# A GRU recurrence inside a fused kernel: state as the stationary operand, W_hh streamed in four column tiles, tanh in place of sigmoid

## The reference, cut to what matters

```python
# layer 0, quantised on both sides
gate = mx_linear(x, w_gate); up = mx_linear(x, w_up)
x1 = x0 + mx_linear(silu(gate) * up, w_down)
# layer 1, the recurrence (B=16, T=256, D=512)
def cell(h, x):
    gi = x @ W_ih + b_ih
    gh = h @ W_hh + b_hh
    r = sigmoid(i_r + h_r); z = sigmoid(i_z + h_z)
    n = tanh(i_n + r * h_n)
    return (1.0 - z) * n + z * h
# layer 1, router: silu hidden layer, top 2 of 16 by softmax, then base + experts
```

## Time and profile before

| | |
|---|---|
| three timed runs | 1957.7, 1959.59, 1968.15 us; median 1959.59 |
| span of the profiled execution, first to last instruction | 1957.8 us (its own time is not listed apart; it is within 2 us of the median) |
| TensorE busy | 1641.2 us (84%) |
| VectorE busy | 1636.9 us (84%) |
| ScalarE, GpSimd busy | 635.5 and 643.7 us (32%, 33%) |
| the 256 steps | 238.4 to 1936.2 us |

### The profile page before, as it was taken

The page is one execution under the profiler, slowest core; times in us unless marked ns, Lnnn a source line. Parts: engine busy times, 40 slices in busy tenths (PEclk is TensorE's granted clock), DMA queues, the critical chain, the costliest instruction groups (busy, mean ns, idle before and its releaser), DMA issues. The chain is left out here.

```text
span 1957.8 us, 82261 instructions
## 1 busy us (share of the span) xinstructions
PE 1641.2 (84%) x32972; PEld 1251.9 (64%) x32972; DVE 1636.9 (84%) x5843; ACT 635.5 (32%) x1711; POOL 643.7 (33%) x795
## 2 busy tenths in 40 slices
PE   5422347999999999999999999999999999999976
PEld 2211115776777777777777777777777777777764
DVE  8999887888888888888888888888888888887653
ACT  1111223433333333333333333333333333333331
POOL 4545323333333333333333332333333333332111
PEclk8755568999999999999999999999999999999997
DMA  7313120000000000000000000000000000000100
GB/s 264 135 59 124 40 97 23 25 30 31 22 19 27 30 30 30 30 30 30 30 30 29 26 30 30 30 30 30 30 30 30 27 17 24 30 25 27 33 14 18
DMA packets 35405, 80.45 MB, mean 41 GB/s; under 512 B 4864, under 2 KB 5248, under 8 KB 34688
## 3 DMA queue, kind: packets, MB, share of 16 engines
q1 hardware_dynamic: 28080, 63.09, 9.6%
q10 hardware_dynamic: 6992, 12.13, 1.8%
HBM read 58.43 MB, written 16.78 MB: 38 GB/s over the span
## 5 line engine op out<-in xcount | busy, mean ns | idle before, releaser
L1294 PE MATMUL ps_rn<-hx,whh 128*128 128x32 f16 x16384 | 451.2, 176 | 85.0 <-DVE hx L715 47.4
L1294 PEld LDWEIGHTS ps_rn<-hx,whh 128*128 128x128 f16 x16384 | 430.9, 96 | 129.8 <-DVE hx L715 90.3
L1016 POOL COPY hT_steps<-hx 128x128 f16<-128x128 f16 x256 | 120.2, 469 | 992.3 <-DVE hx L715 992.3
L1187 PE MATMUL ps_gi<-x1T,wih 128*128 128x128 f16 x4608 | 289.6, 219 | 1.2 <-ACT gi L523 1.2
L1187 PEld LDWEIGHTS ps_gi<-x1T,wih 128*128 128x128 f16 x4608 | 271.3, 98 | 25.9 <-issue 1.7
L532 ACT ACTIVATE r<-r_pre,scale 128x64 f32<-128x64 f32 x256 | 89.0, 348 | 581.6 <-DVE r_pre L735 581.6
L1294 PE MATMUL ps_z<-hx,whh 128*128 128x32 f16 x8192 | 244.2, 176 | 0.0
L1294 PEld LDWEIGHTS ps_z<-hx,whh 128*128 128x128 f16 x8192 | 223.5, 96 | 0.1
L523 ACT ACTIVATE gi<-ps_gi,b_i,scale_x 128x128 f32 (+1 forms) x384 | 144.4, 456 | 159.1 <-PE ps_gi L1187 159.1
L1003 POOL TENSOR_TENSOR qf<-f8c,fe 128x512 bf16<-128x512 bf16 x128 | 135.8, 1061 | 148.4 <-DVE f8c L796 148.4
L1120 PE MATMUL ps_gate_up<-wq,qxT 128*128 128x512 bf16 x512 | 143.6, 397 | 19.5 <-issue 15.0
(11 more groups left out here) (198 smaller groups left out, 2885.2 us busy)
## 6 DMA issues: line engine op xcount, KB each, us to landing
wih<-in_x_steps ACTq DMA_DIRECT2D x32, 256.0 KB, 5.5
xin<-in_x_steps SPq DMA_DIRECT2D x32, 256.0 KB, 4.0
xres<-in_x_steps SPq DMA_DIRECT2D x32, 256.0 KB, 4.1
x_dram<-x SPq DMA_DIRECT2D x32, 256.0 KB, 2.9
x_in<-x_dram SPq DMA_DIRECT2D x32, 256.0 KB, 2.7
out_rows<-y SPq DMA_DIRECT2D x32, 256.0 KB, 2.0
wst<-in_ffn_w SPq DMA_DIRECT2D x12, 512.0 KB, 3.4
sg_gs<-in_ffn_w SPq DMA_DIRECT2D x12, 512.0 KB, 3.7
```

The lines of the kernel that those rows point to most:

```text
L1016: g.tensor_copy(hT_steps[:, :, s, :], hx[:, :, :, :].rearrange("p k u b -> p (k u) b"))\
L1187: last = mm(ps_gi[:, j * P:(j + 1) * P], wih_parts[:, k, at:at + P], x1T[:, x, k, :], start=k + w + x == 0, stop=k == KD - 1 and w == 1)
L1294: last = mm(ps[:, (at + j) * 2 * B:(at + j + 1) * 2 * B], whh[:, k, u, gate * D + j * P:gate * D + (j + 1) * P], hx[:, k, :, :].rearrange( ...
```

## The change

`state_products` swaps the operands. The 32 columns of `hx` for one chunk of depth are now stationary, in one of four groups of 32 columns of TensorE's array, and W_hh streams past: one product writes 32 partitions of the bank, 256 columns for r and n together and 128 for z. That is 32 products for r and n and 32 for z, 64 a step. The sums now lie sequence on partition, in blocks of 32x32, so VectorE turns them with a 32x32 block transpose from PSUM into `rn_turned` and `z_turned` before it adds. The bias of n's recurrent part is laid out beside r's share in `gi`, so that one pair of additions of 128 columns serves r and n.

`sigmoid(a)` becomes `(1 + tanh(a/2)) / 2`, with the halves folded into scales and into `scalar_tensor_tensor` operations. In the recurrence the z sums now stand ahead of `rn` on VectorE, and z's tanh ahead of n's on ScalarE. In the feed-forward net and the router one silu on ScalarE takes the place of a sigmoid on ScalarE and a product on VectorE. The router's softmax share becomes a tanh and two small GpSimd operations. Some buffers of the weight preparation share memory with later ones.

```diff
--- before.py
+++ after.py
+GI_PARTS = 4
+GI_AT = {GATE_N: 0, GATE_Z: 1, GATE_R: 2}
+GI_BIAS = 3
+GROUPS = P // 32
...
-        gi = sb("gi", [P, 2 * 3 * STEPS * HB])
+        gi = sb("gi", [P, 2 * GI_PARTS * D])
         h = sb("h", [P, HB])
         hx = sb("hx", [P, KD, 2, B], F16)
-        r_half, r_pre, z_half, z_pre = (sb(x, [P, HB]) for x in ("r_half", "r_pre", "z_half", "z_pre"))
-        hn_half, hn, r, z = (sb(x, [P, HB]) for x in ("hn_half", "hn", "r", "z"))
-        rn, n_pre, n, n_scaled, nmh, zd = (sb(x, [P, HB]) for x in ("rn", "n_pre", "n", "n_scaled", "nmh", "zd"))
+        rn_turned, z_turned = sb("rn_turned", [P, 2, KD, 2, B]), sb("z_turned", [P, KD, 2, B])
+        rn_half, rn_pre = sb("rn_half", [P, 2, KD, B]), sb("rn_pre", [P, 2, KD, B])
+        z_half, z_pre = sb("z_half", [P, HB]), sb("z_pre", [P, HB])
+        r_tanh, z_tanh, rn, n_pre, n = (sb(x, [P, HB]) for x in ("r_tanh", "z_tanh", "rn", "n_pre", "n"))
+        less_z, zh, zn = (sb(x, [P, HB]) for x in ("less_z", "zh", "zn"))
...
+        def gi_r_and_bias(c, s):
+
+            if isinstance(c, int):
+                at = (c % 2 * GI_PARTS + GI_AT[GATE_R]) * D
+                part = gi[:, at:at + 2 * D]
+            else:
+                part = gi[:, bass.ds((c & 1) * (GI_PARTS * D) + GI_AT[GATE_R] * D, 2 * D)]
+            return part.rearrange("p (q k n) -> p q k n", q=2, k=KD)[:, :, :, s * B:(s + 1) * B]
...
-                    nc.scalar.activation(hid_sg[:, :], hid_pre[:, :], ACT.Sigmoid).then_inc(hs_ok, 1)
+                    nc.scalar.activation(hid[:, :], hid_pre[:, :], ACT.Silu).then_inc(hid_ok, 1)
...
-                    wait(act, gs_done, count(f, NF, s // 2))
-                    nc.scalar.activation(sg[:, :], ps_gate[:, :], ACT.Sigmoid).then_inc(sg_done, 1)
+                    wait(act, inter_done, count(f, NF, s // 2))
+                    nc.scalar.activation(gs, ps_gate[:, :], ACT.Silu).then_inc(gs_done, 1)
...
-                    act.wait_ge(r_pre_ok, t1)
-                    nc.scalar.activation(r[:, :], r_pre[:, :], ACT.Sigmoid, scale=S_INV).then_inc(r_ok, 1)
+                    act.wait_ge(rn_pre_ok, t1)
+                    nc.scalar.activation(r_tanh[:, :], rn_pre[:, 0, :, :], ACT.Tanh, scale=HALF_S_INV).then_inc(r_ok, 1)
+                    act.wait_ge(z_pre_ok, t1)
+                    nc.scalar.activation(z_tanh[:, :], z_pre[:, :], ACT.Tanh, scale=HALF_S_INV).then_inc(z_ok, 1)
                     act.wait_ge(n_pre_ok, t1)
-                    nc.scalar.activation(n[:, :], n_pre[:, :], ACT.Tanh, scale=S_INV).then_inc(n_ok, 1)
-                    act.wait_ge(z_pre_ok, t1)
-                    nc.scalar.activation(z[:, :], z_pre[:, :], ACT.Sigmoid, scale=S_INV).then_inc(z_ok, 1)
+                    nc.scalar.activation(n[:, :], n_pre[:, :], ACT.Tanh, scale=HALF_S_INV).then_inc(n_ok, 1)
...
-                r_both, n_both, z_both = (ps.rearrange("p (k u b) -> p k u b", k=KD, u=2) for ps in
-                                          (ps_rn[:, 0:2 * HB], ps_rn[:, 2 * HB:4 * HB], ps_z[:, 0:2 * HB]))
                 if s == 0:
                     dve.wait_ge(gi_ev, count(c, 3, 3))
                 dve.wait_ge(rn_mm, t1)
-                v.tensor_tensor(by_chunk(r_half[:, :]), r_both[:, :, 0, :], gi_step(c, GATE_R, s),
-                                ALU.add).then_inc(r_half_ok, 1)
-                v.tensor_tensor(by_chunk(hn_half[:, :]), n_both[:, :, 0, :],
-                                b_h[:, 2 * KD:3 * KD].unsqueeze(2).broadcast_to([P, KD, B]),
-                                ALU.add).then_inc(hn_half_ok, 1)
-                dve.wait_ge(r_half_ok, t1)
-                v.tensor_tensor(by_chunk(r_pre[:, :]), r_both[:, :, 1, :], by_chunk(r_half[:, :]),
-                                ALU.add).then_inc(r_pre_ok, 1)
-                dve.wait_ge(hn_half_ok, t1)
-                v.tensor_tensor(by_chunk(hn[:, :]), n_both[:, :, 1, :], by_chunk(hn_half[:, :]),
-                                ALU.add).then_inc(hn_ok, 1)
+                v.transpose(rn_turned[:, :, :, :, :], ps_rn[:, 0:4 * HB]).then_inc(rn_turn_ok, 1)
+                dve.wait_ge(rn_turn_ok, t1)
+                v.tensor_tensor(rn_half[:, :, :, :], rn_turned[:, :, :, 0, :], gi_r_and_bias(c, s),
+                                ALU.add).then_inc(rn_half_ok, 1)
+                dve.wait_ge(rn_half_ok, t1)
+                v.tensor_tensor(rn_pre[:, :, :, :], rn_turned[:, :, :, 1, :], rn_half[:, :, :, :],
+                                ALU.add).then_inc(rn_pre_ok, 1)
                 beside(1)
-                dve.wait_ge(hn_ok, t1)
+                dve.wait_ge(z_mm, t1)
+                v.transpose(z_turned[:, :, :, :], ps_z[:, 0:2 * HB]).then_inc(z_turn_ok, 1)
+                dve.wait_ge(z_turn_ok, t1)
+                v.tensor_tensor(by_chunk(z_half[:, :]), z_turned[:, :, 0, :], gi_step(c, GATE_Z, s),
+                                ALU.add).then_inc(z_half_ok, 1)
+                dve.wait_ge(z_half_ok, t1)
+                v.tensor_tensor(by_chunk(z_pre[:, :]), z_turned[:, :, 1, :], by_chunk(z_half[:, :]),
+                                ALU.add).then_inc(z_pre_ok, 1)
+                dve.wait_ge(rn_pre_ok, t1)
                 dve.wait_ge(r_ok, t1)
-                v.tensor_tensor(rn[:, :], r[:, :], hn[:, :], ALU.mult).then_inc(rn_ok, 1)
-                dve.wait_ge(z_mm, t1)
-                v.tensor_tensor(by_chunk(z_half[:, :]), z_both[:, :, 0, :], gi_step(c, GATE_Z, s),
-                                ALU.add).then_inc(z_half_ok, 1)
+
+                v.scalar_tensor_tensor(by_chunk(rn[:, :]), by_chunk(r_tanh[:, :]), 1.0, rn_pre[:, 1, :, :], ALU.add,
+                                       ALU.mult).then_inc(rn_ok, 1)
                 dve.wait_ge(rn_ok, t1)
-                v.tensor_tensor(by_chunk(n_pre[:, :]), by_chunk(rn[:, :]), gi_step(c, GATE_N, s),
-                                ALU.add).then_inc(n_pre_ok, 1)
-                dve.wait_ge(z_half_ok, t1)
-                v.tensor_tensor(by_chunk(z_pre[:, :]), z_both[:, :, 1, :], by_chunk(z_half[:, :]),
-                                ALU.add).then_inc(z_pre_ok, 1)
+                v.scalar_tensor_tensor(by_chunk(n_pre[:, :]), gi_step(c, GATE_N, s), 2.0, by_chunk(rn[:, :]), ALU.mult,
+                                       ALU.add).then_inc(n_pre_ok, 1)
                 beside(2)
                 wait(dve, hcopy, c * STEPS + s)
 
+                dve.wait_ge(z_ok, t1)
+                v.tensor_scalar(less_z[:, :], z_tanh[:, :], 1.0, HALF_S_H, ALU.subtract, ALU.mult)
+                v.scalar_tensor_tensor(zh[:, :], z_tanh[:, :], 1.0, h[:, :], ALU.add, ALU.mult).then_inc(zh_ok, 1)
+                dve.wait_ge(zh_ok, t1)
                 dve.wait_ge(n_ok, t1)
-                v.scalar_tensor_tensor(nmh[:, :], n[:, :], S_H, h[:, :], ALU.mult, ALU.subtract).then_inc(nmh_ok, 1)
-                v.tensor_scalar(n_scaled[:, :], n[:, :], S_H, None, ALU.mult)
-                dve.wait_ge(nmh_ok, t1)
-                dve.wait_ge(z_ok, t1)
-                v.tensor_tensor(zd[:, :], z[:, :], nmh[:, :], ALU.mult).then_inc(zd_ok, 1)
-                dve.wait_ge(zd_ok, t1)
-                v.tensor_tensor(hx[:, :, 0, :], by_chunk(n_scaled[:, :]), by_chunk(zd[:, :]),
-                                ALU.subtract).then_inc(hx_hi, 1)
-                v.tensor_tensor(h[:, :], n_scaled[:, :], zd[:, :], ALU.subtract).then_inc(h_ok, 1)
+                v.tensor_tensor(zn[:, :], less_z[:, :], n[:, :], ALU.mult).then_inc(zn_ok, 1)
+                dve.wait_ge(zn_ok, t1)
+                v.scalar_tensor_tensor(hx[:, :, 0, :], by_chunk(zh[:, :]), 0.5, by_chunk(zn[:, :]), ALU.mult,
+                                       ALU.subtract).then_inc(hx_hi, 1)
+                v.scalar_tensor_tensor(h[:, :], zh[:, :], 0.5, zn[:, :], ALU.mult, ALU.subtract).then_inc(h_ok, 1)
                 low_part(t1 + 1)
...
-                        dve.wait_ge(sg_done, count(f, NF, s // 2 + 1))
-                        v.tensor_tensor(gs[:, :], ps_gate[:, :], sg[:, :], ALU.mult).then_inc(gs_done, 1)
...
+                    for place, sign in enumerate((0.5, -0.5)):
+                        g.tensor_scalar(share[:, place:place + 1], gap_tanh[:, :], sign, 0.5, ALU.mult,
+                                        ALU.add).then_inc(share_ok, 1)
...
-            def state_products(ps, at, gate):
-
-
-                for j in range(KD):
+            def state_products(ps, gates):
+
+                n = len(gates) * P
+                step = gates[-1] - gates[0] + 1
+                for w in range(2):
                     for k in range(KD):
-                        for u in range(2):
-                            last = mm(ps[:, (at + j) * 2 * B:(at + j + 1) * 2 * B],
-                                      whh[:, k, u, gate * D + j * P:gate * D + (j + 1) * P],
-                                      hx[:, k, :, :].rearrange("p u b -> p (u b)"), start=k + u == 0,
-                                      stop=k + u == KD)
```

(11 more changed lines are left out.)

83 lines of the change are left out of this document (48 added, 35 removed).

## The result

The changed kernel takes 2117.46 us (median of 4 runs, 2115.9 to 2119.9) against 1960.26 of the kernel before, run beside it: a ratio of 1.0799, 95% interval 1.0775 to 1.0824. It is 157 us slower. The forecast said slower, by 55, with a range of 1905 to 2095: the direction came true, the time lies outside the range. One execution among all that follow stands apart, 7475.56 us in run 12, where the nine others took 1949.0 to 1957.7; no cause of it is known, and the ratio given there leaves it out.

What follows compares the result with a forecast made beforehand. TensorE and VectorE were taken to be late in turns, VectorE in steps 3 to 7. Looped tiles +50, written-out tiles +12 and start-up -7 gave +55 on 1959.6, so 2015 us, range 1905 to 2095.

Steps and rivals of the forecast that it cites:

- the steps across the branch: Steps 7 and 0, going by TensorE through the loop's branch: 13.4 us together against 13.91 before.
- the gap between dependent operations: On VectorE, 0.04 us taken between an operation and the one that depends on it.
- What bounds it: TensorE and VectorE late in turns, VectorE in steps 3 to 7; TensorE's products to take 1.0 (r, n) and 0.8 (z).
- One of the signs: In the profile after, VectorE was to be busy above 90% of a looped tile.
- The transposes and the chain: VectorE's turns at 0.42 and 0.28 us, its chain 3.41 from rn_turned to line 715: +0.35 in every step.
- two passes: Rival: each transpose costs 0.26 and 0.14 more per step, 3.2 a tile, 2095 us in all; chance 0.12.
- the column groups did overlap: Rival, that they don't: TensorE's products take 5.1 to 6.1 a step instead of 2.4, 2600 us or more; chance 0.05.
- The waits for GpSimd: VectorE sums with two SBUF inputs held by GpSimd: step 3 7.6 against 6.45, step 7 6.0 against 5.6, step 5 +0.15.
- The rival in which the waits don't come: VectorE's sums are not held by GpSimd: step 3 5.45, a tile 50.9, 1935 us or 1900; chance 0.25.
- The small operations and the router: beside(1)'s operations uncovered, two more GpSimd operations for the share: step 4 6.55 against 5.54, step 6 7.9 against 6.54.
- The sum: A looped tile of 53.7 us against 51.7, +2.0 a tile, over 25 looped tiles +50.
- The start-up: Ahead of the tiles, gs leaves the chain: some 7 us less.

Runs made afterwards that it cites:

- run 12: The changed kernel with all tiles written out instead of looped and the transposes' results in PSUM: 1953.22 us, 0.997 of the kernel before.
- run 10: The changed kernel with its loop over 12 pairs of tiles, so that which half of gi is read is a constant: 2034.98 us, ratio 1.038.
- run 5: The changed kernel with 21 additional one-column memsets at VectorE's start, moving its loop body from 939 to 960 in the instruction stream: 2052.74 us, ratio 1.0479.
- run 1: The changed kernel with both transposes writing to unused columns of their PSUM banks instead of SBUF: 2092.31 us, ratio 1.0678 to the kernel before.
- run 9: The kernel before with 107 additional one-column memsets ahead of VectorE's program, so that its loop body begins at 1067 instead of 960: 1983.14 us, ratio 1.0132.
- run 11: The kernel before, written out, with one silu operation in place of the gate's sigmoid and product: 1856.1 us, 0.9476 of the kernel before.

## Why the prediction was wrong, and what held of it

The direction and most of the mechanism held, the size did not: +157 against +55. In the forecast's own terms, two of them were mis-sized, both by what a hardware loop costs: the steps across the branch, 13.4 forecast and 15.69 measured, which is the larger, and the gap between dependent operations, 0.04 forecast and 0.14 measured behind three operations a step.

**What bounds it.** Right: VectorE is late in nearly all steps, and TensorE's relief pays little. The wait for r and n fell from 106.8 to 22.3 us, and `ps_rn` starts z after 0.88 and ends after 1.06, near the forecast 1.0. z takes 0.5 to 0.6, below the 0.8 that I took and within its bounds. One of the signs failed: VectorE was to be busy above 90% of a looped tile and is busy 84% (919 of 1100 us), since the gaps behind dependent operations and the jump are idle time. Written out it is 92%.

**The transposes and the chain.** Right in length, 0.44 and 0.31 against 0.42 and 0.28, and 3.38 against 3.41 for the chain, but only in the kernel written out. The Trainium skill, "VectorE: DVE Perf Modes", section "The three transpose paths", has 311 ns for 128x128 in bf16; this trace has 306 for fp32, and the runs have nothing in bf16 beside it. There were no two passes, and the column groups did overlap: those rivals are out.

**The first step that failed: "between dependent ones I take 0.04".** That holds (0.034) only where the operation's address is a constant. Where an operation in the loop reads `gi`, 0.14 lie between it and its forerunner, and the change put three such operations one behind another (`rn_half`, `z_half`, `n_pre`). The term is 0.2 to 0.3 in most steps, 1.7 a tile, some 40 us over 25 tiles (run 10 against run 5). No row of the kernel before shows it, since no operation that reads `gi` follows there directly on the one it waits for: `z_half` stands between `rn` and `n_pre`.

**The second and larger one: the steps across the loop's branch, "13.91 - 0.6 - 0.6 + 0.67 = 13.4".** I took the branch as a fixed 1.41 on TensorE that VectorE does not have. In fact each engine has its own, and it is long when the engine fetches its loop anew. The change shortened TensorE's loop from 2080 instructions (130 KB) to 1568 (98 KB); it is no longer fetched anew, and the 1.41 of "issue" ahead of step 0's products is gone. VectorE's shrank too, from 302 to 295, but moved from 960 to 939 in the stream, and has been fetched anew since. Measured: 15.69 for steps 7 and 0, 2.3 above the forecast, and 0.35 more in step 4. With VectorE's loop moved back by 21 instructions they take 13.35, and the kernel 2052.74 (run 5). That 13.35 meets the forecast's 13.4 is in part luck: the forecast went by TensorE through a branch of 1.41, and what was measured is VectorE through a loop without one, with the address gaps in it.

**The waits for GpSimd.** Right in kind and place: 7.6 was forecast for step 3 and 7.83 measured, with three operations held. That the size fits so well is luck, as the three were not the ones I named. `f8c` did not get in ahead of `xg` but came 0.02 late, and so `rn_turned` started 2.5 after the step's beginning and not 1.6, and `z_half` passed free. The rival in which the waits don't come is out by run 1.

**The small operations and the router.** Step 4 was to be 6.55 and step 6 7.9; written out they are 6.31 and 7.79, and the loop adds 0.9 and 0.3; of the 0.9, 0.35 goes with the long jump (run 5). In step 6 two `share` operations of 0.33 on GpSimd stand ahead of `c`, and `wxa` waits 0.55 for `coeff`, which comes behind it.

**The sum.** With VectorE's loop in a short place a tile is 55.0 against the 53.7 forecast: the address term of 1.7 is missing, while the other terms of steps 3 to 6 had been taken 0.06 to 0.24 too long (written out 7.54, 6.31, 6.26 and 7.79 against 7.6, 6.55, 6.5 and 7.9). The sum's 11.75 for steps 1 and 2 was given without its working; it is 12.2 in the loop and 11.45 written out. The start-up, forecast 7 shorter, is 10 shorter at the end of tile 0's first step (330.1 against 339.8 us). Of the 157 us, 92 are left then; the other 65 are the jump. For a full tile written out the forecast had some +3, measured are 3.9 (52.0 against 48.1). The kernel before, without its branch, waits only 63 us for TensorE's r and n instead of 107, so the relief was worth still less there: steps 1 and 2 gain 0.4. Why step 7 alone is 0.8 longer written out is only partly shown: 0.3 of it comes back with the turned sums in PSUM (run 12), and the rest was not tried apart.

## What to carry to other kernels

Relief on one engine is worth what the other engine waits for it, and here that was 107 us at most, of which 43 went away with the loop (63 are left written out); moving the work of turning onto the engine that was already late costs 0.8 us in each of 256 steps. Price a transpose on the late engine before anything that it makes possible elsewhere. In a hardware loop, look at the instruction queues' packets per pass and at "issue" behind the branch and further on in the body, for each engine, before and after: if a loop's body is fetched anew, a few operations of padding, or writing the loop out, may be worth more than the change that is being studied (65 and 81 us here). And ask of a gain whether it lies in the tiles or in the start-up: silu's did so for the larger part.

## What the runs showed of the hardware

- **A loop's body is fetched anew or not by its size and place.** Queue 14, which brings VectorE's instructions, moves 8 KB a packet (1.20 MB in 148), 128 instructions of 64 bytes. Bodies at 960 to 1262, 960 to 1255 and 908 to 1187 stayed; those at 939 to 1234, 1067 to 1362, 940 to 1235 and 1067 to 1369 were fetched anew in each pass. (Places are counted in VectorE's records of the trace from its first, with the 38 records of an earlier loop that runs twice counted once.) All seven fit one rule, found on six of them and then tried on the last (run 9): a body stays if it touches three pieces, and does not if it touches four, with a border 44 to 64 behind a multiple of 128. The number of pieces is not shown apart from the start: the four that did not stay begin 43 or 44 behind a multiple of 128, the three others 12 or 64, so a rule by the start alone fits as well. Five packets come at a turn and not four. On TensorE, with 16 KB a packet, 98 KB stayed and 130 KB did not. The Trainium skill, "Runtime: NRT & Kernel Launch", section "Instruction fetch mechanics", has an instruction memory of 32 KB for most engines and 128 KB for TensorE, and a stall at a taken branch whose target is no longer in it. For TensorE the size and the skill's blocks of 16 KB agree with these runs. VectorE's packets are 8 KB, half of the skill's block, and bodies of 18 to 19 KB, well below its 32 KB, did not stay in some places.
- **The jump costs 1.7 to 2.9 us of idle time on VectorE a pass** (means of six kernels with 147 or 148 packets), 0.3 more in step 4 where the body is the changed one, and 65 us in the whole changed kernel, but only 25 in the kernel before, where TensorE's own fetch lay beside it.
- **An address computed from the loop's counter costs 0.1 us between two dependent VectorE operations** (0.14 against 0.03).
- **A transpose of fp32 on VectorE costs what an ordinary operation of its size does**: 435 ns for 256 columns and 306 for 128, from PSUM to SBUF, where the ordinary ones of 64 and 512 columns (217 and 682 ns) give 416 and 283, an estimate along a straight line; PSUM to PSUM 450 and 321. It is not held by GpSimd: the longest of 256 takes 451.
- **Two tables on ScalarE.** Silu and sigmoid do not share one: each switch is a load of 1.28 us (run 11). Silu and tanh do: two loads in the whole changed kernel.
- **Four column groups side by side**: 32 products of 256 columns in 1.06 us, and 32 of 128 columns in 0.5 to 0.6.
